# Gate logits from x and the attention rows, corrected for the layer norm afterwards, and the gates at the head of VectorE's turn

## The reference

```python
out = out_unnorm / jnp.maximum(norm, 1e-10)      # both from Phi_Q, the exps of query to landmark distances
attn_out = out.reshape(b, n, 256) @ Wo.T + bo
x1 = layernorm(x + attn_out)
gate_logits = x1 @ Wg.T + bg                      # [tokens, 8]
topk_vals, topk_idx = jax.lax.top_k(gate_logits, 2)
gate_w = jax.nn.softmax(topk_vals, axis=-1)
y = sum over the two chosen experts e of gate_w[e] * (x1 @ We[e].T + be[e])
x2 = layernorm(x1 + y)
```

## Time and profile before

| | us |
|---|---|
| median of 3 runs (lowest to highest) | 1580.98 (1577.76 to 1583.66) |
| the profiled execution's own time | 1599.07 |
| its span, first to last instruction | 1597.3 |
| mean granted clock of TensorE, 1.0 being 2.4 GHz | 0.954 |

### The profile page before, as it was taken

How to read it: one execution, slowest core, us unless ns; L and a number is a source line. 1 busy time by engine, 2 the same in 40 slices (tenths; PEclk the granted TensorE clock), 3 DMA queues, 4 the chain that set the end, 5 groups by cost and what they waited for, 6 DMA issues and landing times.

```text
span 1597.3 us, 47451 instructions
## 1 busy us (share of the span) xinstructions
PE 1355.1 (85%) x18232; PEld 1106.1 (69%) x18232; DVE 1108.2 (69%) x3373; ACT 969.4 (61%) x1713; POOL 567.6 (36%) x588
## 2 busy tenths in 40 slices
PE   4698898998998978888888888888876769999995
PEld 3477787887887855555656556555555668999995
DVE  4498873478974357778787877777776656666663
ACT  2466675676766647676767666666653335556554
POOL 2000000000000003465655555656544435666665
PEclk9799998999999979999999999999997889999997
DMA  3878888787789542353333333333324135554442
GB/s 109 142 175 157 183 193 147 146 186 158 170 202 188 124 141 89 100 199 122 122 109 123 110 125 109 123 110 119 122 73 134 55 110 157 166 154 128 139 126 70
DMA packets 179328, 216.21 MB, mean 135 GB/s; under 512 B 59043, under 2 KB 117669, under 8 KB 178341
## 3 DMA queue, kind: packets, MB, share of 16 engines
q1 hardware_dynamic: 165284, 175.15, 44.1%
q0 software_dynamic: 13824, 38.03, 6.6%
HBM read 107.47 MB, written 53.86 MB: 101 GB/s over the span
## 4 chain that ended last, share of the span: by engine, by line
PE 49%; DVE 29%; issue 10%; SPq 4%; DMA 3%; ACT 3%; POOL 1%; DVEq 0%; POOLq 0%; ACTq 0%; another core or an unknown queue 0%
PE bank L350 9%; PE bank L352 8%; PE bank L351 8%; PE bank L1689 3%; PE bank L1705 3%; DVE phi L1244 3%; PE bank L1690 2%; DVE st L1295 2%; DVE phi L1091 2%; PE bank L1955 2%; DVE inversion L1119 2%; PE bank L1925 2%; PE bank L1879 2%; PE bank L1835 2%; PE bank L1850 2%
## 5 line engine op out<-in xcount | busy, mean ns | idle before, releaser
L644 POOL TENSOR_TENSOR xl<-x_raw,xh 128x512 fp32r<-128x512 f32 x60 | 78.8, 1332 | 682.2 <-ACT xh L896 682.2
L872 ACT ACTIVATE phi<-bank,nlt,invt 128x512 f32<-128x512 f32 x256 | 185.3, 785 | 56.6 <-PE bank L1802 54.6
L749 ACT ACTIVATE phi<-bank,invt 128x512 f32<-128x512 f32 x256 | 162.8, 684 | 89.1 <-PE bank L1690 88.9
L665 POOL DMA_INDIRECT rows_dram<-x,place_i x128 | 142.7, 1115 | 136.9 <-DVE place_i L1361 103.8
L683 POOL DMA_INDIRECT out<-phi,tile_to x156 | 152.7, 979 | 51.7 <-issue 37.4
L1689 PE MATMUL bank<-l_hh,k_hl 128*128 128x256 f32 x512 | 146.6, 317 | 27.1 <-DMA k_ha<-key_aug 12.3
L1091 DVE TENSOR_SCALAR phi<-phi,phi_max,phi_min 128x1024 f32<-128x1024 f32 x128 | 103.7, 810 | 89.2 <-ACT phi L749 89.0
L955 ACT ACTIVATE phi<-bank,tile_g 128x256 f32<-128x256 f32 x156 | 71.1, 474 | 136.7 <-PE bank L1955 99.1
L1244 DVE TENSOR_SCALAR phi<-phi,phi_max,phi_min 128x1024 f32<-128x1024 f32 x128 | 104.5, 817 | 64.4 <-ACT phi L872 64.1
L1484 DVE SCALAR_TENSOR_TENSOR phi<-bank,tile_g,phi 128x256 f32<-128x256 f32 x156 | 72.1, 479 | 104.9 <-ACT phi L955 71.3
L1690 PE MATMUL bank<-l_lo,k_ha 128*128 128x256 f32 x512 | 132.7, 290 | 0.0
(11 more groups left out here) (277 smaller groups left out, 4270.8 us busy)
## 6 DMA issues: line engine op xcount, KB each, us to landing
x_raw<-in_xT SPq DMA_DIRECT2D x64, 512.0 KB, 4.4
tile_in<-rows_dram SPq DMA_DIRECT2D x156, 130.0 KB
x_tok<-in_x SPq DMA_DIRECT2D x32, 512.0 KB
attn<-den_dram SPq DMA_DIRECT2D x64, 256.0 KB
k_hl<-attn_h SPq DMA_DIRECT2D x32, 256.0 KB
k_ha<-attn_h SPq DMA_DIRECT2D x32, 256.0 KB
k_hl<-attn_l SPq DMA_DIRECT2D x32, 256.0 KB
k_ha<-key_aug SPq DMA_DIRECT2D x128, 64.0 KB, 3.1
```

The costliest lines, as they stand in the source:

```text
L665: nc.gpsimd.indirect_dma_start(out=rows_dram, out_offset=bass.IndirectOffsetOnAxis(ap=place_i[:, p % 2, t:t + 1].bitcast(u32), axis=0), in ...
L749: nc.scalar.activation(phi[:, n], bank[6 + s][:], ACT.Exp, scale=invt[:]).then_inc(exp_done, 1)
L872: nc.scalar.activation(phi[:, i], bank[4 + i % 4][:], ACT.Exp, bias=nlt[:, c // CPB, i:i + 1], scale=invt[:]).then_inc(qexp_done, 1)
```

## The change

By the layer norm's definition, x1 = (x + attention output) * rs1 + nm1 with one scale and one shift for each token. So the logits of x1 are rs1 times the logits of the unnormalised row, plus nm1 times the sum of the gate weights, plus the bias. The change computes the unnormalised row's logits on PE from two parts: x in its transposed layout (a tile `x_T`, loaded by a new DMA for each chunk) times the gate weights, and the normalised attention rows `attn`, before the projection with Wo, times a product of Wo and the gate weights (`wgo`), made once. The transposes of x1, their copies on ACT and the tile dependence on them go away.

Each of the two parts is 8 matmuls of the kind that there were 8 of. The logits' transpose becomes a matmul with a selecting matrix of 32 columns. DVE reads the logits of chunk p + 1 at the end of turn p (`gates_read`), after the last `normalise`, and scales and shifts them at the start of the next turn (two small instructions), where `gates_begin` and `choices` now stand ahead of the first clamp. POOL makes the shift with two small instructions in `ln1`. `gates_end` and `find_places` move ahead of `normalise_rows`. The ranks move from bank 2 to bank 3, and on PE ahead of `queries(n, 0)`; the gate logits move ahead of the output projection, and are those of chunk p + 1. SP's spread of the inverses also waits for the logits. `denominators` has new waits.

```diff
+        x_T = sb("x_T", [P, KC, CH])
+        gate_in = x_T[:].rearrange("p k n -> p (k n)")[:, 0:KC * (D + P)].rearrange("p (k n) -> p k n", k=KC)
+        wgo = sb("wgo", [P, KC, 32])
+        wg_sum, bo_gate, gate_shift = sb("wg_sum", [P, E]), sb("bo_gate", [P, E]), sb("gate_shift", [P, TPC, E])
...
                 sp.wait_ge(inv_stored, 16 * (c + 1))
+                sp.wait_ge(logits_done, c)
                 for s in range(KC):
                     heads = den_dram[HPS * s:HPS * s + HPS].rearrange("h t n -> h (t n)")
                     sp.dma_start(attn[:, s], rep(heads, 1, HD)).then_inc(inv_spread, 16)
+
+            def load_gate_x(c):
+
+                if absent(c):
+                    return
+                if c == 0:
+                    sp.wait_ge(gate_products, 1)
+                sp.wait_ge(logits_done, c)
+                sp.dma_start(x_T[:], xT_v[:, :, c * CH:(c + 1) * CH]).then_inc(xT_loaded, 16)
 
...
+            sp.dma_start(gate_in, gate_rows.rearrange("(k p) n -> p k n", p=P)).then_inc(gate_loaded, 16)
...
                 store_inverses(a + 1)
                 spread_inverses(a + 1)
+                load_gate_x(a + 1)
...
                 layernorm_coefs(mv1, ve1, rs1, nt1, nm1, slice(0, TPC)).then_inc(ln1_coef, 1)
+                pool.wait_ge(gate_set, 1)
+                pool.wait_ge(ln1_coef, c + 1)
+                own.then(nc.gpsimd.tensor_tensor(gate_shift[:], rep(wg_sum[:], 1, TPC), rep(nm1[:], 2, E), ALU.mult))
+                nc.gpsimd.tensor_tensor(gate_shift[:], gate_shift[:], rep(bg_sb[:], 1, TPC), ALU.add).then_inc(shift_ready, 1)
...
-            def x1_copy(c, tp):
-                if absent(c):
-                    return
-                if c:
-                    act.wait_ge(logits_done, c)
-                act.wait_ge(x1t_done, 2 * c + tp + 1)
-                nc.scalar.activation(x1_T[:, :, tp * 256:tp * 256 + 256].rearrange("p k (t j) -> p t k j", t=2),
-                                     bank[tp][:].rearrange("p (t k j) -> p t k j", t=2, k=KC), ACT.Copy).then_inc(x1c_ready, 1)
...
                 weights_hi(p)
                 for m in EARLY.get(p, ()):
                     tile(m)
-                x1_copy(p + 1, 0)
-                x1_copy(p + 1, 1)
                 q_exps(q + 1, range(0, 2))
                 save_attention(q, 0)
                 q_exps(q + 1, range(2, 4))
+                gate_exp(p + 1)
                 if n > 0:
                     query_hi(n + 1, 1)
-                save_logits(p + 1)
+                save_logits(c + 1)
                 save_attention(q, 1)
                 q_exps(q + 1, range(4, 6))
-                gate_exp(p + 1)
                 if begins_batch(q + 2):
                     z_landmark_major((q + 2) // CPB)
...
+            def gates_read(c):
+
+                if absent(c):
+                    return
+                dve.wait_ge(gate_done, c + 1)
+                logit = bank[2][:, GATES:GATES + TPC * E].rearrange("p (t e) -> p t e", t=TPC)
+                V.tensor_tensor(lg[:], logit, rep(bo_gate[:], 1, TPC), ALU.add).then_inc(gate_read, 1)
+
             def gates_begin(p):
 
                 if absent(p):
                     return
-                dve.wait_ge(gate_done, p + 1)
-                logit = bank[2][:, P:2 * P].rearrange("p (t e) -> p t e", t=TPC)
-                V.tensor_tensor(lg[:], logit[:, :, 0:E], rep(bg_sb[:], 1, TPC), ALU.add).then_inc(gate_read, 1)
                 dve.wait_ge(gate_read, p + 1)
+                dve.wait_ge(shift_ready, p + 1)
+                own.then(V.tensor_tensor(lg[:], lg[:], rep(rs1[:], 2, E), ALU.mult))
+                own.then(V.tensor_tensor(lg[:], lg[:], gate_shift[:], ALU.add))
                 dve.sem_inc(dve_waited, 1)
...
-                rank = bank[2][:, RANKS:RANKS + (TPC + 1) * COMBOS].rearrange("p (t e) -> p t e", t=TPC + 1)
+                rank = bank[3][:, 0:(TPC + 1) * COMBOS].rearrange("p (t e) -> p t e", t=TPC + 1)
...
+            def gate_constants():
+
+                own.then(V.memset(wgo[:], 0.0))
+                dve.wait_ge(gate_products, 1)
+                V.tensor_copy(wgo[:, :, 0:E], bank[2][:, 0:KC * E].rearrange("p (k e) -> p k e", k=KC))
+                V.tensor_copy(wg_sum[:], bank[2][:, KC * E:(KC + 1) * E])
+                V.tensor_copy(bo_gate[:], bank[2][:, (KC + 1) * E:(KC + 2) * E]).then_inc(gate_set, 1)
+
...
+                gates_begin(p)
+                choices(p)
                 q_clamp(q, range(0, 2))
                 residual(c, c % X1)
                 row_stats(c, c % X1)
-                gates_begin(p)
-                choices(p)
+                q_clamp(q, range(2, 4))
+                gates_end(p)
+                find_places(p)
                 normalise_rows(c, c % X1)
-                q_clamp(q, range(2, 4))
+                if p == -4:
+                    gate_constants()
                 if p == -3:
                     own_identity()
                 if p == -2:
                     weights_lo(0)
-                gates_end(p)
-                find_places(p)
                 q_clamp(q, range(4, 6))
                 normalise(a, 0)
                 q_clamp(q, range(6, 8))
                 normalise(a, 1)
                 if begins_batch(q + 1):
                     landmark_values((q + 1) // CPB)
+                gates_read(c)
                 queries_lo(n, 0)
...
                 pe.wait_ge(qphi_ready, PAIRS * c + 4 * half + 4)
-                if c >= 3:
-                    pe.wait_ge(ranks_read, c - 2)
-                else:
-                    pe.wait_ge(den_read, c)
+                pe.wait_ge(den_read, c)
+                if c >= 2:
+                    pe.wait_ge(gate_read, c - 1)
+                pe.wait_ge(gate_set, 1)
...
+                if c >= 3 and half == 0:
+                    pe.wait_ge(ranks_read, c - 2)
...
-                pe.wait_ge(x1c_ready, 2 * p)
-                if p == 0:
-                    pe.wait_ge(ql_done, 8)
+                pe.wait_ge(ql_done, 2 * min(p + 4, NCH))
...
-            def x1_transposes(p, tp):
+            def gate_weights():
+
+                pe.wait_ge(gate_loaded, 16)
+                pe.wait_ge(bo_ready, 1)
+                lefts = [lambda k, s=s: gate_in[:, k, s * P:(s + 1) * P] for s in range(KC)] + [
+                    lambda k: raw(ones_r[:]), lambda k: gate_in[:, k, D:D + P]]
+                for i, left in enumerate(lefts):
+                    for k in range(KC):
+                        last = mm(bank[2][:, E * i:E * (i + 1)], left(k), wg_raw[:, k], start=(k == 0), stop=(k == KC - 1))
+                last.then_inc(gate_products, 1)
+
+            def gate_logits(c):
+
+                if absent(c):
+                    return
+                pe.wait_ge(xT_loaded, 16 * (c + 1))
+                pe.wait_ge(attn_ready, 2 * (c + 1))
+                pe.wait_ge(logits_saved, c)
+                pe.wait_ge(den_read, min(c + 2, NCH))
+                for i, (weights, values) in enumerate(((wg_s, x_T), (wgo, attn))):
+                    for k in range(KC):
+                        for t in range(TPC):
+                            last = mm(bank[2][32 * t:32 * t + 32, 0:P], weights[:, k], values[:, k, t * P:(t + 1) * P],
+                                      start=(i + k == 0), stop=(i + k == KC))
+                last.then_inc(logits_done, 1)
+
+            def logit_transpose(c):
+
+                if absent(c):
+                    return
+                pe.wait_ge(logits_saved, c + 1)
+                mm(bank[2][:, GATES:GATES + TPC * E], logit_rows[:], cst[:, C_SEL:C_SEL + TPC * E], start=True, stop=True).then_inc(gate_done, 1)
+
+            def ranks(p):
 
                 if absent(p):
                     return
-                pe.wait_ge(x1_ready[tp], 2 * (p + 1))
-                pe.wait_ge(ql_done, 2 * min(p + 5, NCH))
-                for t in (2 * tp, 2 * tp + 1):
-                    for k in range(KC):
-                        at = 256 * (t % 2) + 128 * k
-                        last = nc.tensor.transpose(bank[tp][:, at:at + P], x1[p % X1][:, t, k * P:(k + 1) * P], ident)
-                last.then_inc(x1t_done, 1)
-
-            def gate_logits(p):
-
-                if absent(p):
-                    return
-                pe.wait_ge(x1c_ready, 2 * (p + 1))
-                if absent(p + 2):
-                    pe.wait_ge(ranks_read, p)
-                else:
-                    pe.wait_ge(den_read, p + 3)
-                for k in range(KC):
-                    for t in range(TPC):
-                        last = mm(bank[2][32 * t:32 * t + 32, 0:P], wg_s[:, k], x1_T[:, k, t * P:(t + 1) * P],
-                                  start=(k == 0), stop=(k == KC - 1))
-                last.then_inc(logits_done, 1)
-
-            def logit_transpose(p):
-
-                if absent(p):
-                    return
-                pe.wait_ge(logits_saved, p + 1)
```

(36 more changed lines are left out.)

5 lines of the change are left out of this document (added).

## The result

The changed kernel takes **1624.7 us** (median of 4 runs, 1622.6 to 1626.1), the kernel before beside it 1582.3 (4 runs, 1577.8 to 1585.3). The ratio is 1.027, with a 95% interval of 1.024 to 1.030: slower by 42 us, inside the predicted range of 1590 to 1640 and 10 us above the predicted time. The profiled execution took 1626.1 us, like its other runs, while the profiled one of before took 17 us more than its median; so the two spans stand closer together than the two kernels do.

The account below looks back on a forecast made before the run. The prediction took a loop of waits between DVE (12 us) and PE (7) as the bound, no engine being full. Adding +39 for turns, +1 constants and -6 last turns to 1581 gave 1615 us, range 1590 to 1640.

Parts of the forecast that it names:

- The new wait and its holder: Head of PE's turn: the first denominators now wait for `gates_read`, behind all four clamps and both `normalise` on DVE.
- The turn of 19.0 at full clock: Query loop: the new cycle of 9.3 + 9.7 us gives a turn of 19.0 us, as before.
- DVE's gain: DVE in the query loop: the 2.97 us gained by lost waits goes into waiting for denominators, about 2.6 in the trace.
- All idle in one piece: PE in the query loop: all idle time, 3.2 us a turn, stands in one piece ahead of the first denominators.
- The price of the clock: PE behind the pause: half clock in nine turns in ten, mean 1.65 us, so +1.5 us a turn, +39 over 26.
- constants: Before the first turn: 8 tiny matmuls and four DVE operations, 0 to 3 us, taken as +1.
- The last turns, 29 to 31: End of the query loop: marks no longer stand behind residual and statistics, -6 us, bounds 0 and 13.3.
- The sum: Whole kernel: +39 for 26 turns, +1 constants, -6 last turns, +34 us in all.
- the clock holds: Rival, PE's clock in the query loop: it falls seldom or never, 1576 us; chance 13%.
- long falls every turn: Rival, PE behind each pause: half clock for six microseconds, up to 3 us a turn, 1646 us; chance 8%.
- the spread comes late: Rival, inverses' spread: added load and the logits wait delay it, `normalise` waits some tenths a turn, 1625 us; chance 5%.
- VectorE becomes the bound: Rival, query loop: first denominators not late, DVE's work sets a 16.4 us turn, 1508 us; chance 4%.

Follow-up runs that it names:

- e2: Changed kernel with 24 unused matmuls of 256 columns filling PE's pause and the logits' transpose moved behind them; 1604.0 us, ratio 1.011.
- e7: Changed kernel without 31 of its 32 x_T transfers, all logits made from chunk 0's x; 1621.3 us, ratio 1.023.
- e8: Changed kernel with `plan_first` put ahead of `invert_denominators`, where VectorE waits for PE's denominators; 1623.9 us, ratio 1.025.
- e1: Changed kernel with `gates_read(c)` moved up to right behind `find_places(p)`, ahead of `normalise_rows`; 1533.0 us, ratio 0.966.
- e6: Changed kernel with `gates_read(c)` moved up two clamps and a product, right behind the clamps of pairs 4 and 5; 1543.4 us, ratio 0.975.
- e5: Changed kernel with `gates_read(c)` moved up one clamp and one product, right behind `normalise(a, 0)`; 1565.8 us, ratio 0.989.
- e4: Kernel before, with only PE's first-half denominators made to wait until VectorE has clamped all pairs of the chunk; 1707.6 us, ratio 1.077.

## Why the prediction was right, and where it was off

- **The new wait and its holder: right.** PE starts 0.2 us after `gates_read`, and moving that one read up by 1.32 and 1.93 us shortened the turn at full clock by 1.33 and 1.94; by 3.30, by 2.79, and there DVE's own work ends it.
- **The turn of 19.0 at full clock: right**, 19.02 in e2, where DVE's read doesn't wait for the filler in a usual turn. DVE's gain did go into its wait for the denominators; I had 2.6, it is 4.39 with the half clock in it, and at most 2.9 in e2.
- **All idle in one piece: right**, 3.40 us against 3.2, and 4.0 to 4.3 ahead of each batch's first chunk, 1.9 to 2.2 behind most landmark turns, which I had not told apart.
- **The price of the clock: right.** I had 1.65 in nine of ten turns, 1.5 a turn; it was 1.57 behind the pauses of 19 of 24 turns, and 1.44 a turn with all else. +39 was forecast for 26 turns, 1.44 x 26 = 37.5 measured.
- **The first turns: a term left out.** I had +1 for constants; chunks 0 to 4 took 6.1 more. Chunk 1's turn was 15.07 us before and 18.35 after (18.02 in e7 and e8): the turns that had no gates yet were short, and the wait for DVE's end holds there too.
- **The three turns ahead of the last: a term left out.** From chunk 28 to 31 the kernel lost 7.0 us. At 1.44 a turn 4.3 were to be expected. `plan_first` is the rest: before, the turn that it delays took 20.8 us, 1.8 over a usual one; now it takes 25.4, 4.8 over, because the plan stands behind DVE's wait for the denominators. Put into that wait, it gave 3.3 back (e8).
- **The last turns, 29 to 31: right.** I had -6, and it was -8.5. PE's waits for the marks fell there from 9.6 us in three to 5.1 in two (the fourth wait of rows 9, 1.3 us, belongs to turn 28).
- **The sum: near, and in part by luck.** Forecast were 39 + 1 - 6 = 34; the query loop took 47.7 - 8.5 = 39.2 more. The two terms left out, about 5 for the first turns and 3 for the plan, are 8 too few, and the last turns took back 2.5 of them. The other 3 us up to the 42.3 between the medians stand in no stage that I could name.
- **The rivals.** That the clock holds is excluded (0.92). So are long falls every turn: of the 20 in the even stretch 4 lasted 6.8 us, the others 3.4. That the spread comes late is excluded too: in that stretch DVE never waited for it. That the added work costs the time is excluded for the transfers by e7, and for all together by e1, which keeps every added operation and is faster than the kernel before. The rival "VectorE becomes the bound" had its point right, "as soon as X stands 3 us earlier": e1 does that, and its turn is 16.23 where I had written 16.4. Its 1508 was too low by 20 to 25, as its landmark turns take 19 to 26 us and most of the half clock that is left lies in them.

What stays open: what makes one pause of 2.08 us cost the clock and the next not, and the variation of the experts' stage.

## What to carry to other kernels

When a change lets a buffer be freed by an instruction at the end of another engine's turn, look for what waits on that buffer at the head of the next: here one read of 0.18 us, placed 3 us too late, turned a gain of 50 us into a loss of 42. When short waits merge into one, the sum of idle time may stay and the time still grow, because the pause is long enough for TensorE's clock to fall; the merged pause must be priced with what runs right behind it. And a once-only piece of work has a place in the turn that hides it: check it again whenever the waits around it move.

## What the runs showed of the hardware that was not expected

- Idle pieces of PE at the head of a turn, chunks 4 to 28, and how often the clock was at half right behind them: 1.47 to 1.48 us, 0 of 12 (e6); 1.85 to 1.87 us, 1 of 14 (the changed kernel, e7, e8); 2.07 to 2.25 us, 6 of 12 (e5); 2.71 to 3.01 us, 3 of 6 (e5); 3.4 to 4.3 us, 18 of 18 in each of the changed kernel, e7 and e8. A fall costs about 1.6 us in a turn of 19. Between harmless and costly there is no sharp step but a range in which the same pause does either.
- Adding 24 matmuls of 256 columns a turn made the changed kernel 21 us faster (e2).
- Pauses of 4.05 us in the kernel before with the wait alone (e4) brought 6.8 us at half clock in a turn of 23.85; those of 3.40 in the changed kernel 3.4 us in one of 20.59.
